# Row loads that wait for products alone, stores one unit later, biases spread; four output buffers for the gated products

## The chip, the cores and the metric

The kernel runs on one NeuronCore of a Trainium2 chip. The metric is the device time of one execution in microseconds, the median of several runs. The core has five engines that matter here: TensorE (PE) multiplies, VectorE (DVE), ScalarE (ACT) and GpSimd (POOL) do elementwise work, and SyncE (SP) issues all the DMAs of this kernel on one queue. Each engine executes its own instructions in order, and engines wait for each other through semaphores.

## The reference, cut to what matters

The program is one transformer-like layer on 2 x 1024 tokens of width 2048: attention, a gated product with a context, and a large dense product. Two parts of it matter here.

```python
# gated products (the "mlp" stage): g_in, u_in are [tokens, 512], mlp_in_w is [2, 2048, 512]
gate = jnp.einsum('bli,oi->blo', g_in, mlp_in_w[0])
up = jnp.einsum('bli,oi->blo', u_in, mlp_in_w[1])
mlp_out = jax.nn.silu(gate) * up
...
# dense product (the "ffn" stage): x is [2, 1024, 2048], w is [2048, 2048]
w = _dequant(weight_q, scale, zp)          # (q - zp) * scale by groups of 64
x = x + jnp.einsum('bsk,nk->bsn', _layernorm(x), w) + bias
```

All of it is float32. The kernel splits each operand into a rounded high half and the remainder as low half, and forms three products (high by high, high by low, low by high) instead of one.

## The kernel before, in words

The stages follow each other in one program: qkv, attention, write1, the gated products (`build_mlp`, line 2186), write2 (`build_write2`, line 1714) and the dense product (`build_ffn`, line 2473). `build_plane` (line 2407) has no time of its own: it dequantises the weights of the dense product on DVE during the gated products. Each stage gives functions for each engine, and `build_rest` writes them out in order, so that the order on every engine is fixed by hand. Tail and head of two stages overlap through functions with `ahead` in their names.

**Gated products.** There are 64 units. A unit takes 512 tokens (a chunk of four tiles) and 128 output columns, and does 24 matmuls of 128x512: 12 into `psG` (gate) and 12 into `psU` (up), line 2325. Eight units (KS) make a chunk; four chunks are done with the first eight column blocks, then the same four with the other eight. So "chunk 3" below is units 24 to 31. In unit u:

- ACT makes `sil` from `psG` (L2284), then the high halves of rows (`hi_x`, L2258) and weights (`hi_w`, L2247).
- DVE multiplies `psU` by `sil` into `mo` (L2385). This instruction waits until the buffer `mo[u % 2]` is stored, which is the store of unit u-2. Behind it in DVE's queue stand the low halves (`lo_x` L2263, `lo_w` L2251) and the dequantisation of `build_plane` (L2442, L2447, L2455).
- SP's loop (line 2334) goes once per unit: it issues the loads of weights and of rows (`raw`, four tiles for the next chunk, asked for in units 1 to 4 of a chunk, and split by ACT and DVE in the same units 1 to 4), the loads and stores of `build_plane` every third unit, and at the end waits for `mo` of this unit and stores it (L2352).

**Dense product.** A Strassen-like scheme: seven products (steps) of half-size blocks for each of two groups of columns, 14 steps of eight units (`PAIRS`), 112 units in all. Units 0 to 7 are mixed into the tail of write2, units 8 to 111 follow (`SEAM` = 8). One unit is 24 matmuls of 128x512 into `psF[u % 2]` (L2904 to L2906). The rows of a unit are one block or the sum or difference of two blocks of the normalised input; five of the seven steps (1, 2, 4, 5, 6) have two blocks. For such a unit:

- SP loads the first block into `xl[u % 4]` (L2598) and the second into `xs[i % 3]` (L2605), and pieces of the next step's weights (L2615, and L2620 where two are added);
- POOL adds the two blocks (L2859), and two pieces of weights (L2868);
- ACT makes the high half into `xh[u % 3]` (L2738), DVE the low half (`lo_x`, L2787), and the same for pieces (L2748, L2792);
- PE multiplies; DVE adds the product to one or two accumulators (`finish`, L2802, one add for each output cell of the unit).

The order on DVE in iteration u is `finish(u-1)`, `lo_x(u+2)`, pieces. PE starts unit u after `lo_x(u)` and `finish(u-2)`. An accumulator (cell) starts from the residual `x` plus bias: SP loads the residual (`load_base`, L2632), POOL adds the bias (`with_bias`, L2852) three iterations later. After its last unit the cell is stored to `y` (L2639). `base_at` says in which iteration each cell's residual is loaded. SP's loop in this stage (line 2706) sets the order of everything:

```python
for u in range(SEAM, UNITS):
    sp.wait_ge(y_ok, adds[u + 1])      # finish(u) on DVE is done
    ...                                # stores of cells whose last unit is u
    if u + 4 < UNITS:
        load_x(sp, u + 4)              # itself waits for mm_ok, unit u's product
        load_second(sp, u + 4)         # waits for the low half of three sums before
    ...                                # pieces of weights, then residuals
```

Of the kernel before, what the change touches and what calls it, by code (L numbers as in the profile page):

```python
# [19 lines left out]
ALU = mybir.AluOpType  # L20
# [1705 lines left out]
def build_write2(nc, io, k, zone, mlp, stored, cleared):  # L1726
# [8 lines left out]
    with ExitStack() as ctx:  # L1735
# [87 lines left out]
        def scalar_ahead(act, i):  # L1823

            if i == 0:
                act.wait_ge(mlp["mm_u"], 7 * KS)
                act.wait_ge(stored["w_out"], 16 * stored["groups"])
                act.wait_ge(stored["d_out"], 16 * stored["groups"] // 2)
            act.wait_ge(w_in[i % RW], 16 * (i // RW + 1))
            act.activation(wh[:, i * PT:(i + 1) * PT], wraw[:, i % RW], ACT.Copy).then_inc(w_hi, 1)  # L1830

        def vector_ahead(dve, i):

            if i == 0:
                dve.wait_ge(mlp["mm_u"], 7 * KS)
                dve.wait_ge(stored["w_out"], 16 * stored["groups"])
                dve.wait_ge(stored["d_out"], 16 * stored["groups"] // 2)
            if i == RW:
# [346 lines left out]
def build_mlp(nc, io, k, zone, w1, plane):  # L2185


    UNITS = CHUNKS * KM
    with ExitStack() as ctx:
# [5 lines left out]
        mo = sb("m_mo", [P, 2, CH * P])  # L2195
# [16 lines left out]
        mo_out = [sem(f"mo_out{p}") for p in range(2)]  # L2212
# [3 lines left out]
        made = tuple(range(4, 4 + 3 * C * KH, 3))  # L2216

# [115 lines left out]
        def sync(sp, load_w2, load_y):  # L2333
            for u in range(UNITS):
                if u + 4 < KS:
                    load_weights(sp, u + 4)
                if u < UNITS - KS and 1 <= u % KS <= CH:
                    load_reads(sp, CH * (u // KS + 1) + u % KS - 1)
# [13 lines left out]
                sp.dma_start(dst, mo[:, u % 2].rearrange("p (t j) -> p t j", j=P)).then_inc(mo_out[u % 2], 16)  # L2352
            for p in range(2):
                sp.wait_ge(mo_out[p], 16 * UNITS // 2)

# [4 lines left out]
        def scalar(act, hi_w2, hi_y):  # L2360
            for u in range(UNITS):
# [4 lines left out]
                if u < UNITS - KS and 1 <= u % KS <= CH:  # L2366
                    hi_x(act, CH * (u // KS + 1) + u % KS - 1)
# [10 lines left out]
        def vector(dve, lo_w2):  # L2378
            lo_w(dve, 2)
            for u in range(UNITS):  # L2380
                dve.wait_ge(sil_ok, u + 1)
                dve.wait_ge(mm_u, u + 1)
                if u >= 2:
                    dve.wait_ge(mo_out[u % 2], 16 * (u // 2))
                dve.tensor_tensor(mo[:, u % 2], psU[u % 2][:], sil[:, u % 2], ALU.mult).then_inc(mo_ok, 1)  # L2385
                if u + 3 < KS:
                    lo_w(dve, u + 3)
                if u < UNITS - KS and 1 <= u % KS <= CH:
                    lo_x(dve, CH * (u // KS + 1) + u % KS - 1)
# [10 lines left out]
                for i in ahead.get(u, ()):  # L2400
# [3 lines left out]
                    scalar_ahead=scalar_ahead, gpsimd_ahead=gpsimd_ahead, mm_u=mm_u, mo_ok=mo_ok, x_lo=x_lo, w_lo=w_lo)  # L2404


def build_plane(nc, io, k, zone):
# [4 lines left out]
    with ExitStack() as ctx:  # L2412
# [4 lines left out]
        sz = sb("p_sz", [P, RING, 2, H])  # L2417
        diff = sb("p_diff", [P, KH // 2, H])
        q_in = [sem(f"q_in{p}") for p in range(RING)]
# [52 lines left out]
def build_ffn(nc, io, k, zone, w2):  # L2472
# [46 lines left out]
    for j in range(PAIRS):  # L2519
        base_at[0, 0, 1, j] = base_at[0, 1, 1, j] = j - 2 * PAIRS  # L2520
        base_at[0, 0, 0, j] = j + 4
        base_at[0, 1, 0, j] = j + 14
        for half, n in ((0, 1), (1, 0), (0, 0), (1, 1)):
            base_at[1, half, n, j] = last_unit[0, half, n, j] + (4 if (half, n) == (0, 1) else 2)
# [582 lines left out]
```

## Time and profile before

| | us |
|---|---|
| median of 3 runs | 2405.39 |
| lowest, highest | 2388.42, 2405.92 |
| the profiled execution | 2406.18 |
| its span in the trace | 2404.4 |

The profile is of one execution. Busy time is time in which an engine executes; the granted clock of TensorE (PEclk) is given as a share of 2.4 GHz. "Waits" are idle times before an instruction, put down to what ended them. In the chain of waits one walks back from the last instruction to whatever released it. The gated products last from 945.8 to 1349.8 us, units 8 to 111 of the dense product from 1696.2 (start of unit 8) to 2400.6 us (end of unit 111).

### The profile page before, as it was taken

The page shows a single profiled execution, that of the slowest core. Times are in us where ns is not written, and L with a number is a line of the kernel's source. Part 1 is how long each engine was busy: PE and PEld are TensorE (multiplying, and loading weights), DVE is VectorE, ACT ScalarE, POOL GpSimd, SP SyncE. Part 2 cuts the span into 40 slices and gives each one's busy share as a digit, 9 for nine tenths or more (in the row PEclk, how much of TensorE's full clock was granted, in tenths as well). Part 3 has the DMA queues.
Part 4 walks back from the last instruction along what each step waited for, and adds up shares of the span by engine and source line. Part 5 has one row for each costly group of instructions (what it writes and reads, how often), then busy time and mean ns, then how long its engine had stood idle before and what let it go on. Part 6 is the DMA issues. An engine that isn't in the chain of part 4 may idle for free.

```text
span 2404.4 us, 34634 instructions
## 1 busy us (share of the span) xinstructions
PE 2168.2 (90%) x11176; PEld 1745.4 (73%) x11176; DVE 1439.1 (60%) x1950; ACT 1087.3 (45%) x1700; POOL 1179.3 (49%) x717
## 2 busy tenths in 40 slices
PE   6899989999979998997899999998889888989887
PEld 5777756666668887875677889996667666768666
DVE  7778767777647885443544277678545544545443
ACT  3444458888856777221212356665222222222221
POOL 0111159999977775000000387866683675352552
PEclk9999979999988998998899999999999999999999
DMA  5778653333336654766777568789885887675784
GB/s 176 234 239 255 222 148 100 102 93 104 78 104 235 218 209 167 249 210 214 250 246 258 186 254 302 301 292 320 278 286 185 264 279 240 212 258 180 244 258 149
DMA packets 259628, 516.93 MB, mean 215 GB/s; under 512 B 20978, under 2 KB 136690, under 8 KB 240964
## 3 DMA queue, kind: packets, MB, share of 16 engines
q1 hardware_dynamic: 259524, 515.60, 65.3%
q8 instruction: 58, 0.95, 0.2%
q14 instruction: 46, 0.38, 0.0%
HBM read 359.81 MB, written 155.45 MB: 214 GB/s over the span
## 4 chain that ended last, share of the span: by engine, by line
PE 45%; DMA 20%; DVE 13%; issue 7%; ACT 6%; POOL 5%; SPq 4%; DVEq 0%; ACTq 0%; POOLq 0%
DMA s_f_xs<-xnT 9%; PE s_w_psA L1903 5%; PE s_w_psB L1903 5%; DMA s_m_raw<-giT 4%; PE s_psO L922 4%; DMA s_q_xc<-xP 4%; PE s_psS L868 4%; POOL s_f_xs L2859 3%; PE s_m_psG L2325 3%; PE s_m_psU L2325 3%; PE s_psF L2904 3%; PE s_psF L2906 3%; PE s_psF L2905 3%; PE s_psX L899 3%; DMA mlpT<-s_m_mo 2%
## 5 line engine op out<-in xcount | busy, mean ns | idle before, releaser
L2859 POOL TENSOR_TENSOR s_f_xs<-s_f_xl,s_f_xs 128x1024 f32<-128x1024 f32 x80 | 194.5, 2432 | 303.6 <-DMA s_f_xs<-xnT 303.6
L1053 POOL TENSOR_TENSOR s_a_pl<-s_a_pf,s_a_ph 128x1024 fp32r<-128x1024 f32 x128 | 301.9, 2393 | 21.8 <-ACT s_a_pf L1010 21.7
L2787 DVE TENSOR_TENSOR s_f_xl<-s_f_xs,s_f_xh 128x1024 fp32r<-128x1024 f32 x80 | 102.8, 1286 | 306.0 <-ACT s_f_xh L2738 306.0
L2073 POOL TENSOR_TENSOR s_w_yl<-s_w_y,s_w_yh 128x1024 fp32r<-128x1024 f32 x32 | 76.0, 2399 | 414.6 <-ACT s_w_yh L1983 414.6
L2738 ACT ACTIVATE s_f_xh<-s_f_xs 128x1024 fp32r<-128x1024 f32 x80 | 84.8, 1060 | 421.5 <-POOL s_f_xs L2859 421.5
L948 DVE TENSOR_REDUCE s_a_mx<-s_psS 128x1 f32<-128x512 f32 (+2 forms) x248 | 179.3, 754 | 97.2 <-PE s_psS L876 96.7
L2904 PE MATMUL s_psF<-s_f_wh,s_f_xh 128*128 128x512 f32 x448 | 184.1, 411 | 48.0 <-DVE s_f_acc L2802 40.3
L2905 PE MATMUL s_psF<-s_f_wl,s_f_xh 128*128 128x512 f32 x448 | 181.8, 406 | 0.0
L2906 PE MATMUL s_psF<-s_f_wh,s_f_xl 128*128 128x512 f32 x448 | 181.6, 405 | 0.0
L1007 ACT ACTIVATE s_a_ph<-s_psX 128x1024 fp32r<-128x1024 f32 (+1 forms) x160 | 150.6, 941 | 51.5 <-PE s_psX L904 47.8
L449 POOL TENSOR_TENSOR s_q_qk<-s_q_ra,s_q_rb 128x1024 f32<-128x1024 f32 x16 | 37.8, 2360 | 270.7 <-DVE s_q_rb L692 270.7
L2802 DVE TENSOR_TENSOR s_f_acc<-s_f_acc,s_psF 128x512 f32<-128x512 f32 x192 | 124.0, 680 | 45.1 <-PE s_psF L2906 44.9
L2904 PEld LDWEIGHTS s_psF<-s_f_wh,s_f_xh 128*128 128x128 f32 x448 | 87.1, 194 | 79.7 <-issue 45.6
L2904 PE MATMUL s_psF<-s_f_whB,s_f_xh 128*128 128x512 f32 x336 | 136.0, 405 | 3.6 <-DVE s_f_wlB L2792 3.6
L922 PE MATMUL s_psO<-s_a_ph,s_a_vs 128*65 128x512 f32 (+3 forms) x384 | 128.4, 350 | 7.4 <-POOL s_a_pl L1053 7.4
L2905 PE MATMUL s_psF<-s_f_wlB,s_f_xh 128*128 128x512 f32 x336 | 135.0, 402 | 0.0
L2906 PE MATMUL s_psF<-s_f_whB,s_f_xl 128*128 128x512 f32 x336 | 134.9, 401 | 0.0
L1010 ACT ACTIVATE s_a_pf<-s_psX 128x1024 f32<-128x1024 f32 x128 | 131.0, 1023 | 0.0
L2852 POOL TENSOR_TENSOR s_f_acc<-s_f_acc,s_f_fb 128x512 f32<-128x512 f32 x64 | 112.2, 1766 | 36.5 <-DMA s_f_acc<-x 24.8
L868 PE MATMUL s_psS<-s_a_k,s_a_q 96*128 96x512 f32 x372 | 116.4, 401 | 10.3 <-DVE s_a_mx L948 10.0
L922 PE MATMUL s_psO<-s_a_pl,s_a_vs 128*65 128x512 f32 (+3 forms) x384 | 125.3, 338 | 0.0
L2385 DVE TENSOR_TENSOR s_m_mo<-s_m_psU,s_m_sil 128x512 f32<-128x512 f32 x64 | 44.1, 689 | 99.9 <-DMA mlpT<-s_m_mo 42.7
(335 smaller groups left out, 6337.9 us busy)
## 6 DMA issues: line engine op xcount, KB each, us to landing
s_f_xl<-xnT SPq DMA_DIRECT2D x112, 512.0 KB, 5.2
s_f_xs<-xnT SPq DMA_DIRECT2D x80, 512.0 KB, 6.4
s_q_xt<-xT SPq DMA_DIRECT2D x16, 1024.0 KB, 7.7
s_q_xc<-xP SPq DMA_DIRECT2D x16, 1024.0 KB, 9.7
hsD<-s_q_hs SPq DMA_DIRECT2D x16, 1024.0 KB, 4.9
s_w_hin<-hsD SPq DMA_DIRECT2D x16, 1024.0 KB, 5.0
hs<-s_w_res SPq DMA_DIRECT2D x16, 1024.0 KB, 3.9
s_m_raw<-giT SPq DMA_DIRECT2D x32, 512.0 KB, 5.9
```

The costliest lines, as they stand in the source:

```text
L868: pe.matmul(psS[:, at:at + n], qa[0:K3, p, qi * P:(qi + 1) * P], ka[0:K3, p, kk:kk + n], start=True, stop=not last)
L922: mm = pe.matmul(psO[0:VW, half, 512 - n:512], vs[:, r, ki, :], part[:, r, at:at + n], start=(ki == 0 and part is ph), stop=(ki == (3, 7)[ ...
L948: dve.tensor_reduce(mx[:, slot % 2, qi:qi + 1], psS[:, off:off + (qi + 1) * P], AX, ALU.max).then_inc(mx_ok, 1)
L1007: act.activation(ph[:, r, at:at + wide[j]], src, ACT.Exp, scale=scale).then_inc(exp_ok, 1)
L1010: act.activation(full, src, ACT.Exp, scale=scale).then_inc(exp_ok, 1)
L1053: pool.tensor_tensor(pl[:, r, cols], pf[:, j - 1], ph[:, r, cols], ALU.subtract).then_inc(pl_ok, 1)
L1903: mm = pe.matmul(bank[:, 0:n], a[:, p, kt], b[:, kt, cols], start=False, stop=(kt == KM - 1 and a is yl))
L2325: mm = pe.matmul(bank[u % 2][:], a[:, kt], b[:, :, kt], start=(i == 0 and a is w[m][0] and b is xh), stop=(i == KH - 1 and a is w[m][1]))
L2859: pool.tensor_tensor(xs[i % 3][:], xl[u % 4][:].bitcast(F32), xs[i % 3][:], ALU.add if product(u)[1][1][2] > 0 else ALU.subtract).then_inc ...
L2904: pe.matmul(out[:], xh[u % 3][:, kt], high(q, kt), start=(kt == 0), stop=False)
L2905: pe.matmul(out[:], xh[u % 3][:, kt], low(q, kt), start=False, stop=False)
L2906: mm = pe.matmul(out[:], xl[u % 4][:, kt], high(q, kt), start=False, stop=(kt == HK - 1))
```

## The change

In the gated products `mo` becomes four buffers instead of two for units 0 to 51 (`WIDE`), of which two lie in the region of `build_plane`, whose small buffer `p_sz` moves; the last 12 units use two. ACT's and DVE's first use of that region in write2 waits for the stores from these two buffers. Rows for the next chunk are asked for in units 0, 1, 3, 4 of a chunk and split in units 2, 3, 5, 6.

In the dense product SP's iteration u first issues the rows of unit u+4 and the pieces, then waits for `finish(u-1)`, stores the cells whose last unit is u-1, and loads residuals. `base_at` is given anew: the residuals of cells (0,1,0,j) are asked for in iteration 21+j instead of 14+j, and those of group 1 in 45+j, 51+j, 54+j and 77+j instead of 12+j, 50+j, 42+j and 34+j. The ring of semaphores of residuals goes from 8 to 6 and that of stores from 4 to 3. The bias row is loaded ahead of the first two residuals.

```diff
@@ build_write2, scalar_ahead and vector_ahead (the same two lines in each)
                 act.wait_ge(stored["d_out"], 16 * stored["groups"] // 2)
+                for out in mlp["spare_out"]:
+                    act.wait_ge(out, 16 * mlp["spare"])
@@ build_mlp
     UNITS = CHUNKS * KM
+    WIDE = UNITS - 12
...
-        mo = sb("m_mo", [P, 2, CH * P])
+        mo = [sb(f"m_mo{n}", [P, CH * P]) for n in range(2)]
+        mo += [shelf(nc, "s4_", zone["E"] + (28 + 2 * n) * 1024, zone["end"])(f"m_mo{n + 2}", [P, CH * P]) for n in range(2)]
...
-        mo_out = [sem(f"mo_out{p}") for p in range(2)]
+        mo_out = [sem(f"mo_out{p}") for p in range(4)]
+
+        asked, split = (0, 1, 3, 4), (2, 3, 5, 6)
...
+        def place(u):
+
+            return u % 4 if u < WIDE else u % 2
+
+        sent = [0]
+        for u in range(UNITS):
+            sent.append(sum(place(v) == place(u + 1) for v in range(u + 1)))
@@ build_mlp, sync
-                if u < UNITS - KS and 1 <= u % KS <= CH:
-                    load_reads(sp, CH * (u // KS + 1) + u % KS - 1)
+                if u < UNITS - KS and u % KS in asked:
+                    load_reads(sp, CH * (u // KS + 1) + asked.index(u % KS))
...
-                sp.dma_start(dst, mo[:, u % 2].rearrange("p (t j) -> p t j", j=P)).then_inc(mo_out[u % 2], 16)
+                sp.dma_start(dst, mo[place(u)][:].rearrange("p (t j) -> p t j", j=P)).then_inc(mo_out[place(u)], 16)
@@ build_mlp, scalar (and vector alike, with lo_x)
-                if u < UNITS - KS and 1 <= u % KS <= CH:
-                    hi_x(act, CH * (u // KS + 1) + u % KS - 1)
+                if u < UNITS - KS and u % KS in split:
+                    hi_x(act, CH * (u // KS + 1) + split.index(u % KS))
@@ build_mlp, vector
-                if u >= 2:
-                    dve.wait_ge(mo_out[u % 2], 16 * (u // 2))
-                dve.tensor_tensor(mo[:, u % 2], psU[u % 2][:], sil[:, u % 2], ALU.mult).then_inc(mo_ok, 1)
+                if sent[u]:
+                    dve.wait_ge(mo_out[place(u)], 16 * sent[u])
+                dve.tensor_tensor(mo[place(u)][:], psU[u % 2][:], sil[:, u % 2], ALU.mult).then_inc(mo_ok, 1)
@@ build_plane
-        sz = sb("p_sz", [P, RING, 2, H])
         diff = sb("p_diff", [P, KH // 2, H])
+        sz = shelf(nc, "s7_", zone["E"] + 36 * 1024, zone["end"])("p_sz", [P, RING, 2, H])
@@ build_ffn
-        base_at[0, 1, 0, j] = j + 14
-        for half, n in ((0, 1), (1, 0), (0, 0), (1, 1)):
-            base_at[1, half, n, j] = last_unit[0, half, n, j] + (4 if (half, n) == (0, 1) else 2)
+        base_at[0, 1, 0, j] = 3 * PAIRS + j - 3
+        base_at[1, 0, 1, j] = STEPS * PAIRS + j - 11
+        base_at[1, 1, 1, j] = STEPS * PAIRS + j - 5
+        base_at[1, 0, 0, j] = STEPS * PAIRS + j - 2
+        base_at[1, 1, 0, j] = (STEPS + 3) * PAIRS + j - 3
...
-    RB, RY, RW = 8, 4, 5
+    RB, RY, RW = 6, 3, 5
@@ build_ffn, sync_ahead, i == 1
+                sp.dma_start(fb[0][:].rearrange("p c n -> p (c n)"), io["fbias"][:, 0:2 * H]).then_inc(fb_in, 16)
                 load_base(sp, bases[0])
                 load_base(sp, bases[1])
-                sp.dma_start(fb[0][:].rearrange("p c n -> p (c n)"), io["fbias"][:, 0:2 * H]).then_inc(fb_in, 16)
@@ build_ffn, sync
-            for u in range(SEAM, UNITS):
-                sp.wait_ge(y_ok, adds[u + 1])
-                for cell in touched(u):
-                    if last_unit[cell] == u:
-                        store(sp, cell)
+            for u in range(SEAM, UNITS + 1):
                 if u + 4 < UNITS:
                     load_x(sp, u + 4)
                     load_second(sp, u + 4)
-                for n in pieces(u):
-                    load_piece(sp, n)
+                if u < UNITS:
+                    for n in pieces(u):
+                        load_piece(sp, n)
+                if u > SEAM:
+                    sp.wait_ge(y_ok, adds[u])
+                    for cell in touched(u - 1):
+                        if last_unit[cell] == u - 1:
+                            store(sp, cell)
                 for cell in bases[24:]:
                     if base_at[cell] == u:
                         load_base(sp, cell)
             for r in range(RY):
-                sp.wait_ge(y_out[r], 16 * len(stores) // RY)
+                sp.wait_ge(y_out[r], 16 * len(range(r, len(stores), RY)))
```

## Rows read from the trace of the kernel before

**Rows 1.** The page, part 1: busy time, share of the span and instructions by engine

```profile
PE 2168.2 (90%) x11176; PEld 1745.4 (73%) x11176; DVE 1439.1 (60%) x1950; ACT 1087.3 (45%) x1700; POOL 1179.3 (49%) x717
```

**Rows 2.** Waits of PE and DVE, gated products (940 to 1355 us): total, times, longest

```profile
PE s_m_psG L2325 <- ACT s_m_sil L2284: 29.3, 7, 13.0
...
DVE s_m_mo L2385 <- DMA mlpT<-s_m_mo: 42.7, 7, 9.4
```

**Rows 3.** Chain of waits in the gated products: start, us, what

```profile
1110.34 12.00 DMA s_m_raw<-giT
...
1148.44 11.69 DMA mlpT<-s_m_mo
```

**Rows 4.** Windows, gated products: us, PE, PEld, DVE, ACT, POOL busy, PEclk, DMA share, GB/s

```profile
994.50:1038.00 43.50, 43.50 (x194) 36.02 (x193) 23.26 (x18) 8.81 (x12) 0.00 (x0) 1.00 0.69 228
1038.00:1084.50 46.50, 44.06 (x193) 35.87 (x192) 20.96 (x18) 8.46 (x12) 0.00 (x0) 1.00 0.67 212
1084.50:1208.70 124.20, 97.28 (x386) 77.87 (x386) 57.54 (x47) 24.71 (x32) 0.00 (x0) 0.88 0.73 239
1208.70:1306.30 97.60, 89.52 (x386) 72.97 (x385) 46.23 (x38) 17.04 (x24) 0.00 (x0) 0.98 0.69 229
```

**Rows 5.** Waits of PE in the dense product (1696 to 2404 us)

```profile
PE s_psF L2904 <- DVE s_f_acc L2802: 72.8, 40, 5.2
```

**Rows 6.** Chain of waits in the dense product, one turn of the loop

```profile
2112.55 0.34 SPq L2639
...
2112.93 0.43 SPq L2598
...
2113.40 6.07 DMA s_f_xs<-xnT
...
2119.60 2.40 POOL s_f_xs L2859
...
2122.02 1.07 ACT s_f_xh L2738
...
2123.11 0.86 DVE s_f_xl L2787
...
2124.26 0.68 DVE s_f_wl L2792
2124.94 1.21 DVE s_f_acc L2802 x2
```

**Rows 7.** Windows, dense product: the same columns as rows 4

```profile
1696.20:1817.40 121.20, 98.22 (x388) 75.25 (x386) 58.89 (x55) 28.14 (x34) 95.91 (x52) 0.94 0.82 273
1817.40:1862.20 44.80, 44.80 (x194) 35.90 (x193) 24.56 (x32) 13.27 (x17) 9.87 (x5) 1.00 0.53 175
1862.20:2036.30 174.10, 147.96 (x577) 114.66 (x576) 83.29 (x90) 39.62 (x48) 110.45 (x57) 0.93 0.81 262
2036.30:2081.10 44.80, 44.80 (x193) 36.10 (x193) 28.02 (x32) 12.66 (x16) 13.26 (x7) 1.00 0.63 204
2081.10:2187.60 106.50, 94.22 (x386) 73.31 (x386) 49.93 (x59) 27.10 (x32) 58.02 (x30) 0.97 0.74 247
2187.60:2232.80 45.20, 44.80 (x194) 35.78 (x192) 24.25 (x30) 12.65 (x16) 5.04 (x2) 1.00 0.45 151
2232.80:2400.60 167.80, 141.46 (x576) 108.94 (x576) 68.91 (x81) 33.46 (x38) 75.26 (x38) 0.98 0.74 224
```

**Rows 8.** The same view for units 8 to 11 alone

```profile
1696.20:1728.80 32.60, 26.03 (x100) 20.25 (x97) 13.41 (x13) 6.88 (x9) 18.65 (x11) 0.90 0.84 291
```

**Rows 9.** Tile xs in the dense product: issue to landing of its loads and others

```profile
DMA to landing us min/median/max: 4.5/6.4/9.1
```

**Rows 10.** POOL in one unit of step 2, in order of time

```profile
1791.84 1.28 POOL L2868 TENSOR_TENSOR s_f_ws<-s_f_wl,s_f_ws 128x512 f32<-128x512 f32 x1
1793.09 3.97 POOL L2852 TENSOR_TENSOR s_f_acc<-s_f_acc,s_f_fb 128x512 f32<-128x512 f32 x2
```

**Rows 11.** DMA issues: count, KB each, median us to landing

```profile
s_f_acc<-x SPq DMA_DIRECT2D x64, 256.0 KB, 6.9
```

More of the change, by code:

```diff
@@ L1837, in vector_ahead @@
                 dve.wait_ge(stored["d_out"], 16 * stored["groups"] // 2)
+                for out in mlp["spare_out"]:
+                    dve.wait_ge(out, 16 * mlp["spare"])
             if i == RW:
@@ L2351, in sync @@
                 dst = io["mlpT"].rearrange("t p f -> p t f")[:, CH * chunk:CH * (chunk + 1), ds((KS * half + m) * P, P)]
-                sp.dma_start(dst, mo[:, u % 2].rearrange("p (t j) -> p t j", j=P)).then_inc(mo_out[u % 2], 16)
+                sp.dma_start(dst, mo[place(u)][:].rearrange("p (t j) -> p t j", j=P)).then_inc(mo_out[place(u)], 16)
             for p in range(2):
-                sp.wait_ge(mo_out[p], 16 * UNITS // 2)
+                sp.wait_ge(mo_out[p], 16 * (WIDE // 4 + (UNITS - WIDE) // 2))
+                sp.wait_ge(mo_out[2 + p], 16 * WIDE // 4)
         def tensor(pe):
@@ L2382, in vector @@
                 dve.wait_ge(mm_u, u + 1)
-                if u >= 2:
-                    dve.wait_ge(mo_out[u % 2], 16 * (u // 2))
-                dve.tensor_tensor(mo[:, u % 2], psU[u % 2][:], sil[:, u % 2], ALU.mult).then_inc(mo_ok, 1)
+                if sent[u]:
+                    dve.wait_ge(mo_out[place(u)], 16 * sent[u])
+                dve.tensor_tensor(mo[place(u)][:], psU[u % 2][:], sil[:, u % 2], ALU.mult).then_inc(mo_ok, 1)
                 if u + 3 < KS:
                     lo_w(dve, u + 3)
-                if u < UNITS - KS and 1 <= u % KS <= CH:
-                    lo_x(dve, CH * (u // KS + 1) + u % KS - 1)
+                if u < UNITS - KS and u % KS in split:
+                    lo_x(dve, CH * (u // KS + 1) + split.index(u % KS))
                 if 1 <= u - (CHUNKS - 1) * KS < KS:
@@ L2403, in build_mlp @@
         return dict(sync=sync, tensor=tensor, scalar=scalar, vector=vector, sync_ahead=sync_ahead, tensor_ahead=tensor_ahead,
-                    scalar_ahead=scalar_ahead, gpsimd_ahead=gpsimd_ahead, mm_u=mm_u, mo_ok=mo_ok, x_lo=x_lo, w_lo=w_lo)
+                    scalar_ahead=scalar_ahead, gpsimd_ahead=gpsimd_ahead, mm_u=mm_u, mo_ok=mo_ok, x_lo=x_lo, w_lo=w_lo, spare_out=mo_out[2:], spare=WIDE // 4)
 def build_plane(nc, io, k, zone):
```

## The prediction

> **What bounds the kernel now.** I read the page first: TensorE is busy for 90% of the span and nothing else for over 73% [rows 1]. That points to PE, but PE busy is not PE at its rate, so the next view is the windows, cut at the units' own borders. In the dense product the steps whose units load a single block of rows take 44.8 us for eight units, with PE busy all the time at clock 1.00: 5.6 us a unit is PE's own rate there. The steps with two blocks take 121.2 us for two steps, 174.1 for three, 106.5 for two and 167.8 for three, 569.6 us for ten steps or 7.12 us a unit [rows 7]. So 569.6 - 10 x 44.8 = 121.6 us lie above PE's rate. In the gated products an undisturbed chunk takes 43.5 us, and units 8k to 8k+7 of chunks 3 and 4 together 124.2 instead of 87 [rows 4].
>
> The third view says who holds PE. In the dense product PE waits 72.8 us in 40 waits for `finish` on DVE [rows 5], but an add of 0.6 us is not slow: the chain of waits shows what it stands behind. One turn goes: store of `y` 0.34, load of rows 0.43, landing of the second block 6.07, sum on POOL 2.40, high half on ACT 1.07, low half on DVE 0.86, piece 0.68, `finish` 1.21, and then SP issues again, 13.6 us after the turn began [rows 6]. It serves two units: `finish(u)` stands on DVE behind `lo_x(u+2)`, SP asks for the rows of unit u+4 only after `finish(u)`, and these must be through `lo_x(u+4)` before `finish(u+2)`. A turn of 13.6 us for two units is 6.8 a unit, where PE needs 5.6. This latency loop, not the rate of any engine, bounds the two-block steps. The rest of the 121.6 us, beside the waits, is PE at the lower clock after stalls (0.93 to 0.98 in these windows, 1.00 in the others) [rows 7].
>
> In the gated products PE waits for `sil` 29.3 us, and DVE waits 42.7 us in seven waits for the store of `mo` two units before [rows 2]. The chain alternates between two transfers, loads of `raw` and stores of `mo`, which take up to 12.0 and 11.7 us to land [rows 3]; a unit is 5.44 us.
>
> **The change, part by part: gated products.** Four buffers: `mo(u)` waits for the store of u-4, issued three to four units (16 to 22 us) before, against a landing of up to 11.7 [rows 3]. The wait goes for units up to 51; from unit 52 it is back to two units (10.9 us), and a late store can still cost 1 to 2 us. Rows of the next chunk are split two units later than asked for: issue just after `mo(u-1)`, `hi_x` behind the gate of unit u+2, so 2.5 units or 13.6 us against 12.0. What was behind the stalled DVE instruction (SP's wait for `mo`, hence its next loads) comes free with it. What is late next: in chunk 3 SP's load of weights waits for `lo_w` of two before, and `hi_w` uses it one and a half units after. And the DMA engines: chunks 3 and 4 moved 239 GB/s x 124.2 us = 29.7 MB at a busy share of 0.73, so 327 GB/s at full share [rows 4]; the same bytes need 91 us, more than PE's 87. I take 97 for the two (bounds 91 and 124). The 46.5 us of chunk 2 become 44, the 97.6 us of chunks 5 and 6 become 89 [rows 4]. Gain 27.2 + 2.5 + 8.6 = 38 us; bounds 10 (only the stores' waits outside chunk 3 go) and 48. DVE and ACT do the same work. The moved buffer and the waits in write2 cost nothing: they are for stores landed four units before.
>
> **Dense product, the loads.** SP now asks for unit u+4 when product u ends. It needs 0.43 issue + 6.4 landing (the median, [rows 9]) + 2.40 + 1.07 + 0.86 [rows 6] and some 0.3 between, 11.5 us, and has three units, 16.8 us. The loop is cut, with 5.3 us to spare: landings up to 11.7 us are hidden, and the longest of before was 9.1 [rows 9]. SP's new wait, `finish(u-1)` at the end of iteration u, has queued behind it the stores of u-1, the residuals, and the loads of iteration u+1. These last need product u+1, later than `finish(u-1)` in any case, so it costs nothing while `lo_x(u+1)` is in time. A store one unit later costs nothing: the accumulator's next residual comes at least two iterations after it. The tail keeps its order (last product, `finish`, store): 0.
>
> **The residuals spread.** In step 2 two residuals came per unit, and POOL did 2.40 for the sum [rows 6], 1.28 for the piece and 3.97 for two biases [rows 10], 7.65 us per unit against PE's 5.6: there POOL itself was the bound. With none of them in step 2, POOL has 3.7. They now stand in steps with one block of rows, where POOL is idle most of the time (9.87 busy in 44.8, [rows 7]), and in steps 5 and 6, where sum, bias of 2.0 and at most one piece make 5.7. The first use of a cell is three to eleven units after its load; a landing of 6.9 [rows 11] is hidden. The ring of six: in write2's last tile the seventh residual waits for the first to land, which holds the four pieces and the rows behind it for 0 to 2 us; the queue drains meanwhile, and I take 0.5 against a bias row about 1 us earlier: 0 together.
>
> **What the bytes allow.** I counted the DMAs SP issues per step: of units loading two blocks, 2 x 0.52 MB of rows, up to two pieces of 0.26 and one store of 0.26, 1.84 MB a unit; residuals before made it 2.10. For steps 1 to 13 of the new order this is 14.4, 11.0, 10.2, 14.4, 14.9, 13.6, 11.5, 14.4, 11.0, 10.2, 14.4, 13.6, 6.3 MB. The windows give between 224/0.74 = 303 and 273/0.82 = 333 GB/s at full share [rows 7]. At 303 the heavy steps need 47.5 to 49.2 us, at 333 43 to 45. I take the low end, since they come near full share. Three light steps (2, 9, 13) at 46, three of 14.4 MB (4, 8, 11) at 48, step 5 at 50, two of 13.6 at 46.5: 138 + 144 + 50 + 93 = 425. Step 1 keeps its first four units, 32.6 us [rows 8]: their rows are asked for before this loop or fall in the crowd of the stage's end; the other four take 5.7 each: 55.4. Together 480.4 against 569.6, a gain of 89.2; bounds 70 (28 lost to the DMA engines and new stalls) and 112 (all at PE's rate but step 1's head).
>
> The Trainium skill would have it otherwise. By "HBM Reference", section "Specifications (TRN2)", a core has about 358 GB/s of HBM bandwidth; 1.84 MB in 5.6 us is 329 GB/s, so the DMA engines would bind in no step. The heavy steps would then be at 46 like the light ones, an estimate of 11 us less in all. The trace stands against it with 303 to 333 at full share [rows 7].
>
> **Sum.** 2406.2 (the profiled execution's own time) - 38 - 89.2 = 2279; it lies 0.8 above the median of the runs, so 2278 against 2405.4.
>
> **The rivals.**
> - A, the DMA engines cap it: no group of steps has held more than 273 GB/s [rows 7]. If 280 were all they can hold, 14.4 MB need 51.4, 14.9 MB 53.2, 13.6 MB 48.6: 18 us more, and chunks 3 and 4 need 106, 9 more: 2305. At 260 GB/s (held by the ten steps on the mean) nearly 2340. For it: landings grow with the crowd. Against: shares of 0.74 to 0.82, not 1.
> - B, in the gated products the loop through weights takes the place of the one removed: SP waits for `lo_w`, `hi_w` for the landing, and chunk 3 stays as it is. The gain there is 10: 2306. For it: 12.0 us landing [rows 3] against 8 us of lead. Against: behind a late `hi_w` PE still has over a unit in hand.
> - C, slower: with loads asked for up to three units ahead, more of them share the engines and each lands later. It is slower than before only when (landing + 5.1)/3 exceeds 7.12 us, a landing of 16.3 where the median was 6.4; at 18 a unit takes 7.7, 80 units 46 us more, and without the gated products' gain 2452. Against: the bytes are fewer in the crowded steps, and the same engines carried 1.84 MB per turn of 6.8 us.
> - D, the store wait still holds SP in some place I have not seen, and the change does nothing: 2405.
>
> **How the numbers follow.** Forecast (2255 to 2295) 0.60; A 0.22; B 0.10; C 0.03; D 0.05. A measurement of this kernel tells about 1% from no change, 24 us. Forecast, A and B are faster by more than 1%: 0.92; D within: 0.04 and a hundredth of it slower with C: 0.04. The range takes the best case (48 + 112 lies at 2246) nearly whole and A up to 2325: 2250 to 2325.
>
> **What would show it.** Right: windows of two-block steps of 46 to 50 us with clock 1.00; PE's waits for `finish` in the dense product under 20 us, from 72.8; SP's loads of rows within 1 us of a product's end; median landing of `xs` up from 6.4 to 7 to 9; no DVE wait for stores of `mo` before unit 52; chunks 3 and 4 in 97 us; DMA share 0.9 or more in heavy steps; the kernel outside both stages unchanged to 3 us. Wrong: landings over 12 us with PE still waiting 50 us (A); waits of ACT for `wraw` in chunk 3 (B); PE waiting at POOL's biases in steps 0 of the second group, where they now stand.

## The result and the profile after

| | before | after |
|---|---|---|
| median, us | 2405.65 | 2254.32 |
| lowest, highest | 2388.42, 2412.37 | 2246.93, 2257.58 |
| runs | 4 | 4 |
| the profiled execution | 2406.18 | 2254.39 |
| its span | 2404.4 | 2252.3 |

The ratio is 0.9377, with a 95% interval of 0.9323 to 0.9431: 151 us faster, where 127 had been forecast. The time lies inside the range and just below the forecast's own (2255 to 2295).

The page of the changed kernel, part 1 and the first line of part 4, answers [rows 1]:

```profile
PE 2123.3 (94%) x11176; PEld 1724.2 (77%) x11176; DVE 1452.6 (64%) x1950; ACT 1087.4 (48%) x1700; POOL 1180.6 (52%) x717
...
PE 69%; DVE 10%; DMA 8%; issue 5%; ACT 5%; POOL 2%; SPq 1%; DVEq 0%; ACTq 0%; POOLq 0%
```

The instruction counts are those of before; nothing was removed but waiting. The chain that ends last is now PE for 69% and DMA for 8%; on the page of before those two stood at 45% and 20%.

**Where the 152 us of span went.** The start of the gated products came 2.7 us earlier (945.8 to 943.1), they take 355.3 us instead of 404.0 (48.7 less), from their end to the first unit of the dense product it is 283.1 against 283.0, units 0 to 7 take 63.8 against 63.4, and units 8 to 111 take 603.4 instead of 704.4 (101.0 less). So the kernel outside the two stages is unchanged to 3 us, and the two stages gained more than forecast by 10.7 and 11.8 us.

**Gated products.** The windows of chunks 0, 1, 3, 4, 5, 6 and 7 in the changed kernel, with the columns of [rows 4]:

```profile
943.10:993.70 50.60, 48.40 (x200) 39.42 (x201) 17.89 (x19) 20.80 (x30) 0.00 (x0) 0.93 0.54 175
993.70:1037.30 43.60, 43.60 (x194) 36.09 (x194) 23.25 (x18) 8.58 (x12) 0.00 (x0) 1.00 0.73 237
1080.80:1124.30 43.50, 43.50 (x193) 36.03 (x192) 30.05 (x25) 14.49 (x18) 0.00 (x0) 1.00 0.91 306
1124.30:1167.80 43.50, 43.50 (x193) 36.05 (x192) 26.50 (x21) 10.79 (x14) 0.00 (x0) 1.00 0.98 341
1167.80:1211.30 43.50, 43.50 (x193) 36.04 (x192) 22.18 (x18) 8.58 (x12) 0.00 (x0) 1.00 0.85 271
```
```profile
1211.30:1254.80 43.50, 43.50 (x193) 36.03 (x193) 24.45 (x20) 8.58 (x12) 0.00 (x0) 1.00 0.74 248
1254.80:1298.30 43.50, 43.50 (x193) 36.03 (x193) 18.45 (x22) 17.27 (x19) 4.76 (x2) 1.00 0.65 214
```

Seven of the eight chunks are at 43.5 us with PE busy all the time and the clock at 1.00, including chunks 3 and 4, which stood at 124.2 us together with the clock at 0.88 [rows 4]. The row to remember is the fourth: 341 GB/s at a DMA share of 0.98, and PE without a stall.

The waits of PE and DVE in the gated products (940 to 1305 us) of the changed kernel answer [rows 2]; DVE has more rows, of these the first two and the store's:

```profile
PE s_m_psG L2341 <- issue: 4.5, 1, 4.5
PE s_w_psT L1389 <- DVE s_w_yn L1647: 2.1, 1, 2.1
```
```profile
DVE s_m_mo L2402 <- issue: 105.7, 44, 4.5
DVE s_m_mo L2402 <- PE s_m_psU L2341: 37.2, 10, 4.8
...
DVE s_p_diff L2472 <- DMA wD<-s_p_diff: 8.5, 2, 5.0
```

PE's wait for `sil` is gone, and so is DVE's wait for the store of `mo`. DVE still idles before `mo`: 37.2 us of it end with the product, which is PE's own pace, and to 105.7 us the profile puts no releaser ("issue"). Transfers did not get quicker. The tiles `raw` and then `mo`, issue to landing, same stretch, answer [rows 3]:

```profile
DMA to landing us min/median/max: 3.6/5.8/10.7
...
DMA to landing us min/median/max: 2.3/5.2/12.1
```

A store that takes 12.1 us still happens; with four buffers it no longer ends a wait.

**Dense product.** The windows of steps 1, 2, 4, 5, 6 and 12 in the changed kernel, then of all units 8 to 111; columns as before, they answer [rows 7]:

```profile
1645.30:1702.40 57.10, 48.97 (x194) 37.91 (x193) 29.89 (x29) 13.65 (x17) 44.48 (x22) 0.94 0.89 313
1702.40:1749.00 46.60, 45.23 (x192) 35.90 (x193) 28.47 (x27) 15.14 (x18) 33.41 (x18) 1.00 0.81 260
1793.80:1838.40 44.60, 44.60 (x193) 35.94 (x192) 23.96 (x31) 12.38 (x15) 29.63 (x16) 1.00 0.94 311
1838.40:1884.30 45.90, 45.04 (x193) 35.83 (x192) 27.34 (x32) 13.44 (x17) 31.99 (x17) 1.00 0.97 321
1884.30:1933.00 48.70, 46.52 (x194) 37.05 (x193) 33.13 (x27) 13.92 (x18) 34.84 (x18) 0.96 0.91 300
2158.20:2203.90 45.70, 44.87 (x193) 35.86 (x192) 29.47 (x32) 12.83 (x17) 31.36 (x17) 1.00 0.95 322
...
1645.30:2248.70 603.40, 588.95 (x2498) 469.61 (x2496) 348.69 (x374) 167.02 (x201) 367.75 (x189) 0.99 0.83 276
```

The heavy steps 4, 5 and 12 are within about 1 us of PE's 44.8 while the DMA engines are busy for 0.94 to 0.97. What is left above PE's rate stands in step 1 (12 us), step 2 (2) and step 6 (4).

The waits of PE (1645 to 2252 us) answer [rows 5], those of SP show who releases it, and the last line, tile `xs` from issue to landing, answers [rows 9]:

```profile
PE s_psF L2925 <- DVE s_f_acc L2823: 11.9, 8, 3.8
```
```profile
SPq L2617 <- PE s_psF L2927: 271.8, 79, 7.1
...
SPq L2658 <- DVE s_f_acc L2823: 28.6, 21, 5.2
```
```profile
DMA to landing us min/median/max: 4.5/6.8/11.1
```

SP's load of rows (L2617) now stands 79 times behind a product. The rows of a two-block unit u+4 are asked for 0.03 to 0.08 us after the end of product u, but for units 12 and 13 (4.6 and 0.9 us); before it was 7.9 us at the median and 14.2 at most. The landing's median rose only from 6.4 to 6.8, its longest from 9.1 to 11.1, which the prediction's 11.7 still covers.

### The profile page after: what moved, and what is told of

The parts are those of the page before. It is cut to its first block, busy times and chain, and to the rows that moved or that the text cites. A ratio compares the mean times of both kernels' runs of the same rounds, so it can differ in the third digit from the quotient of the medians.

```text
span 2252.3 us, 34615 instructions
## 1 busy us (share of the span) xinstructions
PE 2123.3 (94%) x11176; PEld 1724.2 (77%) x11176; DVE 1452.6 (64%) x1950; ACT 1087.4 (48%) x1700; POOL 1180.6 (52%) x717
## 4 chain that ended last, share of the span: by engine, by line
PE 69%; DVE 10%; DMA 8%; issue 5%; ACT 5%; POOL 2%; SPq 1%; DVEq 0%; ACTq 0%; POOLq 0%
PE s_m_psG L2341 8%; PE s_m_psU L2341 8%; PE s_psF L2925 7%; PE s_psF L2926 7%; PE s_psF L2927 7%; PE s_w_psA L1907 5%; PE s_w_psB L1907 5%; PE s_psO L922 4%; DMA s_q_xc<-xP 4%; PE s_psS L868 4%; PE s_psX L899 3%; DVE s_a_mx L948 1%; DMA s_f_xs<-xnT 1%; PE s_w_psT L1939 1%; PE s_w_psR L1406 1%
## 5 line engine op out<-in xcount | busy, mean ns | idle before, releaser
L2880 POOL TENSOR_TENSOR s_f_xs<-s_f_xl,s_f_xs 128x1024 f32<-128x1024 f32 x80 | 203.7, 2546 | 165.4 <-DMA s_f_xs<-xnT 165.4
L2077 POOL TENSOR_TENSOR s_w_yl<-s_w_y,s_w_yh 128x1024 fp32r<-128x1024 f32 x32 | 76.1, 2404 | 365.9 <-ACT s_w_yh L1987 365.9
L2925 PE MATMUL s_psF<-s_f_wh,s_f_xh 128*128 128x512 f32 x448 | 178.7, 399 | 9.7 <-DVE s_f_acc L2823 8.6
L2300 ACT ACTIVATE s_m_sil<-s_m_psG 128x512 f32<-128x512 f32 x64 | 38.2, 597 | 228.8 <-PE s_m_psG L2341 228.7
L2873 POOL TENSOR_TENSOR s_f_acc<-s_f_acc,s_f_fb 128x512 f32<-128x512 f32 x64 | 102.4, 1612 | 69.5 <-DMA s_f_acc<-x 69.4
L2402 DVE TENSOR_TENSOR s_m_mo<-s_m_psU,s_m_sil 128x512 f32<-128x512 f32 x64 | 44.1, 690 | 143.0 <-issue 105.7
```

Source lines behind the costliest of these rows:

```text
L2880: pool.tensor_tensor(xs[i % 3][:], xl[u % 4][:].bitcast(F32), xs[i % 3][:], ALU.add if product(u)[1][1][2] > 0 else ALU.subtract).then_inc ...
L2925: pe.matmul(out[:], xh[u % 3][:, kt], high(q, kt), start=(kt == 0), stop=False)
```

## The experiments

Two theories on why the time fell further than forecast. **Latency**: both stages were bound only by how early a transfer was asked for; the DMA engines have no limit near these loads, so that once nothing waits, everything goes at PE's rate. **Rate** (the prediction's term, and rival A): the engines give out at 303 to 333 GB/s, and the heavy steps stay above PE's rate for it. The runs also ask which part of the change brought what. Stage times are read from the windows of each run: the stages ahead, which no experiment touches, scatter (the gated products start between 943 and 954 us), so a window is sharper than a whole time. A window scatters too: the changed loop of the dense product took 598.1 to 603.4 us for units 8 to 111 in the five traces that have it (the change and runs 2, 5, 6 and, but for the place of the store, 7). So a difference under some 5 us in that stage tells nothing, unless it stands in one step that is alike in the others.

**1. The gated products alone.** The changed kernel with the dense product of before.

```diff
-            for u in range(SEAM, UNITS + 1):
+            for u in range(SEAM, UNITS):
+                sp.wait_ge(y_ok, adds[u + 1])
...                                 # and base_at, fb[0], stores as before; rings at 6 and 3
```

> The change in the gated products alone (the dense product as before, but with the two semaphore rings at 6 and 3). Theory: the two parts are independent; this keeps the gated products' 355 us and gives back the dense product's 100.8 us: 2254 + 101 = 2355. Rival (a faster stage before pushes the dense product into another crowd of transfers): outside 2345 to 2365. The smaller rings alone cost under 2 us.

2364.48 us (ratio 0.9827, 0.977 to 0.9884). The whole time is at the upper end of what was expected. The gated products take 353.0 us, units 8 to 111 706.0, with the smaller rings in them against 704.4 without. One stretch as long as a chunk (its end of chunk 3 and most of chunk 4) carried more than any in the changed kernel:

```profile
1124.00:1167.50 43.50, 43.50 (x193) 36.02 (x193) 26.38 (x24) 10.74 (x14) 0.00 (x0) 1.00 1.03 351
```

So the gated products' gain is this part's alone, and 351 GB/s, with the DMA engines busy without a gap (their share can read a little over 1), still does not slow PE.

**2. The dense product alone.** The kernel before with `build_ffn` of the changed one.

```diff
-        base_at[0, 1, 0, j] = j + 14
+        base_at[0, 1, 0, j] = 3 * PAIRS + j - 3
...                                 # all of build_ffn; build_mlp, build_plane as before
```

> The change in the dense product alone, gated products as before. Theory: 2254 + 48.7 = 2303, gated products 404 us, dense product from unit 8 about 604 us. Rival (the parts help each other): the two gains, this one's and that of the gated products alone, sum to less than 140 us instead of 151.

2300.76 us (0.9569, 0.9525 to 0.9613); units 8 to 111 take 599.0, the gated products 401.0, with chunks 3 and 4 at 122.0. By windows the parts alone gain 51.0 and 105.4 us in their own stages, the whole change 48.7 and 101.0: by these the two parts add, and neither needs the other. The expectation asked for whole times (under 140 us together would mean that they help each other), and these do not settle it: the two ratios give 145 us together where the whole change gave 150, the medians of that session (2399.03 for the kernel before) give 133, and the intervals of the two ratios are 14 and 11 us to each side.

**3. The loads wait for `finish` again.** Only SP's order is undone; residuals stay spread.

```diff
-            for u in range(SEAM, UNITS + 1):
+            for u in range(SEAM, UNITS):
+                sp.wait_ge(y_ok, adds[u + 1])
+                for cell in touched(u):
+                    if last_unit[cell] == u:
+                        store(sp, cell)
...                                 # and no wait for finish(u-1), no store behind the loads
```

> The changed kernel, but SP's loads of rows wait for finish(u) again, with the store ahead of them as before; residuals stay spread. Theory (the latency loop of 13.6 us per two units is the bound): nine two-block steps go back to 6.8 us a unit, 54 us a step instead of 45.6 on the mean, so 75 to 85 us slower than the changed kernel: 2329 to 2339, PE's waits for finish at 50 us or more. Rival (the spread residuals and their bytes did most of it): under 2290.

2336.71 us (0.9713, 0.9669 to 0.9756). Waits of PE from 1654 us on, the landings of `xs`, and the windows of steps 4 and 5:

```profile
PE s_psF L2923 <- DVE s_f_acc L2821: 65.5, 41, 5.3
```
```profile
DMA to landing us min/median/max: 4.5/6.3/8.4
```
```profile
1813.80:1864.20 50.40, 45.78 (x193) 35.42 (x192) 24.96 (x32) 11.90 (x15) 26.54 (x14) 1.00 0.83 271
1864.20:1920.80 56.60, 48.27 (x193) 36.59 (x193) 25.34 (x32) 13.55 (x16) 30.63 (x16) 0.97 0.83 262
```

With this one wait in SP's loop PE's waits are back (40 before, 41 here), though each transfer lands sooner than in the changed kernel (6.3 against 6.8) and the engines are busy for only 0.83. That is latency, not rate. Units 8 to 111 take 685.4: the order of the loads alone is worth 82.0 us of the stage.

**4. The residuals as before.** Only `base_at` is undone.

```diff
-        base_at[0, 1, 0, j] = 3 * PAIRS + j - 3
+        base_at[0, 1, 0, j] = j + 14
...                                 # and the four of group 1
```

> The changed kernel with the residuals asked for where they were before (14+j, 12+j, 50+j, 42+j, 34+j); loads wait for products alone. Theory: step 2 is bound by POOL at 7.65 us a unit, 61 us instead of 46.6; steps 4 and 5 carry 16.3 MB, at 333 GB/s 49 us instead of 44.6 and 45.9; step 6 2 us less: together 20 us slower, 2274. Rival (transfers capped at 303 GB/s, as the prediction took it): steps 4 and 5 at 54 us, 2283 or more. Rival (POOL's turns are hidden by the longer lead): under 2262.

2266.26 us (0.9425, 0.9387 to 0.9464); units 8 to 111 take 613.7, 10.3 more, of which 7.5 in step 2 and 4.5 in step 5. Windows of steps 2, 4 and 5, and the landings of `xs` in step 5:

```profile
1708.80:1762.90 54.10, 46.35 (x192) 35.52 (x193) 29.00 (x26) 14.39 (x17) 54.10 (x30) 1.00 0.78 278
1807.70:1852.30 44.60, 44.60 (x193) 35.78 (x192) 25.91 (x30) 11.85 (x14) 33.64 (x17) 1.00 0.96 331
1852.30:1902.70 50.40, 46.66 (x193) 35.45 (x192) 32.83 (x32) 13.56 (x16) 50.40 (x25) 1.00 1.01 345
```
```profile
DMA to landing us min/median/max: 5.9/6.7/7.4
```

In steps 2 and 5 POOL is busy for the whole window: 54.10 of 54.10 and 50.40 of 50.40. That is the bound that the prediction had worked out for step 2 (7.65 us a unit with two biases), though only part of the step has two: the four units 19 to 22 take 7.52 to 7.54 us each. In step 5 the DMA engines are full as well, at 345 GB/s; but the landings there are no longer than elsewhere (6.7), so it is POOL that holds this step. The expectation was too high by 8 us: it had step 2 at 61 us, as if all eight units had two biases, and it had put a price on the bytes of step 4 (49 us), which is at PE's rate at 331 GB/s.

**5. Two output buffers, rows as in the change.**

```diff
-            return u % 4 if u < WIDE else u % 2
+            return u % 2
...                                 # and the last waits for the stores, to match
```

> The changed kernel with mo in two buffers again, rows still asked for and split at the new places. Theory: the stores of mo were late because they stood among the loads in a crowd, and up to 12.1 us against 10.9 us of room; with rows early, DVE waits for a few stores, each stall partly taken up by the unit that PE has in hand: 3 to 12 us slower, 2257 to 2266. Rival (the two buffers were the main wait of that stage): 25 us or more slower.

2262.13 us (0.9394, 0.9339 to 0.9449). The gated products take 364.3 us, 9.0 more. The stall of 8.5 us at unit 32 and 2.5 us after it cost 11.0; against that chunk 0 took 48.6 us here and 50.6 in the profile of the change. Chunk 0 does so with the same code too: 48.3 to 48.6 us in four traces, 50.3 to 50.6 in five. So the two buffers are worth 11.0. DVE's row of waits for the store (948 to 1313 us):

```profile
DVE s_m_mo L2401 <- DMA mlpT<-s_m_mo: 24.6, 5, 8.4
```

DVE waits 24.6 us in five waits and PE loses 11.0: the total of such a row is no price, since DVE has cover of its own. That holds for the 42.7 us in [rows 2] as well.

**6. Rows asked for and split as before, four buffers kept.**

```diff
-        asked, split = (0, 1, 3, 4), (2, 3, 5, 6)
+        asked, split = (1, 2, 3, 4), (1, 2, 3, 4)
```

> The changed kernel with four buffers, rows of the next chunk asked for and split in units 1 to 4 as before. Theory: raw rows land up to 12 us after issue and are wanted within half a unit, DVE and ACT stand on them, chunk 3 worst: 20 to 35 us slower, 2274 to 2289. Rival (the stores' wait was the main one): under 2262.

2292.16 us (0.9512, 0.9462 to 0.9562), 3 us beyond what was expected. The gated products take 390.2, 34.9 more, chunk 3 alone 65.5. PE's wait and two of ACT's (954 to 1345 us):

```profile
PE s_m_psG L2341 <- ACT s_m_sil L2300: 20.4, 7, 12.1
```
```profile
ACT s_m_xhXA L2274 <- DMA s_m_raw<-giT: 76.8, 12, 17.6
ACT s_m_xhXB L2274 <- DMA s_m_raw<-giT: 74.1, 16, 11.0
```

ACT waits for rows that have not landed, 17.6 us at the longest (7.0 and 0.4 in all in the changed kernel), and the next `sil` stands behind that `hi_x`. So of the change's two edits in this stage, the room between load and split did most (34.9), the buffers the smaller part (11.0).

The trace of before had the same waits of ACT (940 to 1355 us), about as long:

```profile
ACT s_m_xhXB L2258 <- DMA s_m_raw<-giT: 81.5, 16, 11.7
ACT s_m_xhXA L2258 <- DMA s_m_raw<-giT: 78.7, 12, 17.6
```

DVE stood behind these high halves for 54.0 and 51.4 us there, 14.9 at the longest, against the 42.7 us (9.4 at the longest) for stores that [rows 2] shows.

**7. Stores ahead of the loads.** SP waits for `finish(u-1)` and stores first, then asks for rows.

```diff
+                if u > SEAM:
+                    sp.wait_ge(y_ok, adds[u])
+                    ...                    # stores
                 if u + 4 < UNITS:
                     load_x(sp, u + 4)
...                                 # the same wait and stores are gone behind the pieces
```

> The changed kernel, but in each iteration SP first waits for finish(u-1) and stores the cells of u-1, then loads the rows of u+4 and pieces; residuals last as now. Theory: finish(u-1) is nearly always over when product u ends, so only the place in the queue changes: 0 to 4 us slower, 2254 to 2258. Rival (what matters is that 0.26 MB of store no longer stand ahead of the rows): 10 us or more slower.

2257.15 us (0.9363, 0.9308 to 0.9418), units 8 to 111 600.7: no difference. What mattered is which `finish` SP waits for, u-1 instead of u, not whether it stands before or after the loads.

**8. One unit less of lead.** When product u ends, SP asks for the rows of u+3 instead of u+4.

```diff
-                if u + 4 < UNITS:
-                    load_x(sp, u + 4)
-                    load_second(sp, u + 4)
+                if SEAM < u < UNITS - 3:
+                    sp.wait_ge(mm_ok, u + 1)
+                    load_x(sp, u + 3)
+                    load_second(sp, u + 3)
```

> The changed kernel, but iteration u issues the rows of unit u+3 instead of u+4, after product u. Theory: the way from issue to low half is 11.5 to 12.5 us at the median landing of 6.8 us, and the room is now two units, 11.2 us; so two-block units take on the mean 0.5 to 1.5 us more: 35 to 100 us slower, 2290 to 2355. Rival (the DMA engines' rate, not the lead, sets the remaining distance to PE's rate): under 2275.

2347.81 us (0.9741, 0.9683 to 0.9798). Waits of PE, the landings, and units 8 to 111:

```profile
PE s_psF L2926 <- DVE s_f_acc L2824: 70.5, 35, 5.1
```
```profile
DMA to landing us min/median/max: 4.4/6.3/11.2
```
```profile
1649.20:2345.50 696.30, 619.02 (x2499) 483.85 (x2497) 332.05 (x374) 166.73 (x201) 362.67 (x189) 0.95 0.74 239
```

92.9 us of the stage's 101 are gone with one unit of lead. The way of a pair of blocks took 11.5 us in the prediction's sum, and two units are 11.2: at two there is nothing to spare, at three 5.3 us. Between those two lies nearly the whole gain. This is the plainest evidence for latency: same bytes, same instructions, and a DMA share of 0.74.

**9 to 11. What is left, at the seam.** In step 1 of the changed kernel PE stalls 3.95 and 3.25 us at units 10 and 11 for rows asked for late, and units 13 to 15 take 6.15 to 6.29 us each. The timeline of POOL there, and of DVE beside it (start, us, instruction):

```profile
1681.63 2.86 POOL L2880 TENSOR_TENSOR s_f_xs<-s_f_xl,s_f_xs 128x1024 f32<-128x1024 f32 x1
1684.44 1.29 POOL L2889 TENSOR_TENSOR s_f_ws<-s_f_wlB,s_f_ws 128x512 f32<-128x512 f32 x1
1685.69 2.29 POOL L2873 TENSOR_TENSOR s_f_acc<-s_f_acc,s_f_fb 128x512 f32<-128x512 f32 x1
```
```profile
1685.61 1.23 DVE L2808 TENSOR_TENSOR s_f_xl<-s_f_xs,s_f_xh 128x1024 fp32r<-128x1024 f32 x1 [2.20 <-ACT s_f_xh L2759]
1686.75 1.77 DVE L2813 TENSOR_TENSOR s_f_wlB<-s_f_ws,s_f_whB 128x512 fp32r<-128x512 f32 x1
1688.45 1.27 DVE L2823 TENSOR_TENSOR s_f_acc<-s_f_acc,s_psF 128x512 f32<-128x512 f32 x2
```

POOL goes without a gap from 1681.63 to 1687.98, one sum, one piece, one bias: POOL bounds these units. Three kernels try both ends. The first adds the biases of group 0 earlier, out of these units, and loads the second bias row in iteration 28; the second asks for the rows of units 10 and 11 ahead of SP's wait for the last tile of write2; the third does both.

```diff
-            with_bias(pool, bases[16])
+            for b in range(16, 20):
+                with_bias(pool, bases[b])
...                                 # 20 to 23 in units 8 to 10
@@ sync_ahead, i == 3, out of i == 4 and sync
+                load_x(sp, 10)
+                load_second(sp, 10)
...
+                load_x(sp, 11)
+                load_second(sp, 11)
```

> The changed kernel; POOL adds the biases of the cells (0,0,0,j) earlier (four before unit 8's sums instead of one, two in iteration 8, one each in 9 and 10), and the second bias row is loaded in iteration 28 instead of ahead of unit 11's rows. Theory (POOL at 6.3 us a unit binds units 12 to 16): step 1 falls from 57.1 to 52 to 54, step 2 by about 1: 4 to 6 us faster, about 2249. Rival (DVE or the landings of 9 to 16 us in those units bind anyway): within 2 us of the changed kernel.

> The changed kernel, but the rows of units 10 and 11 are issued ahead of SP's wait for the last tile of write2 (about 9 us earlier). Theory: the stalls of 3.95 and 3.25 us before units 10 and 11 and the lower clock after them go: 7 to 11 us faster, 2244 to 2247, unless POOL at 6.3 us a unit takes part of it back: then 4 to 7. Rival (POOL binds from unit 10 on): under 3 us.

> Both of these edits together. Theory: they remove one bound after the other, so their gains add: 11 to 16 us faster than the changed kernel, 2238 to 2243, step 1 at 46 to 48 us. Rival (one of the two hides the other): no more than the better of the two alone.

| | median, us | ratio, 95% | units 8 to 111 | step 1 | step 2 |
|---|---|---|---|---|---|
| the change | 2254.32 | 0.9377, 0.9323 to 0.9431 | 603.4 | 57.1 | 46.6 |
| biases earlier | 2252.85 | 0.9382, 0.9341 to 0.9423 | 595.6 | 55.2 | 45.1 |
| rows earlier | 2245.28 | 0.9341, 0.9285 to 0.9398 | 594.6 | 51.4 | 46.6 |
| both | 2250.19 | 0.9368, 0.933 to 0.9405 | 592.0 | 51.1 | 44.6 |

Step 1, which takes 57.0 to 57.4 us in the five traces named above, is shorter by 1.9, 5.7 and 6.0 us, and step 2 by 1.5 us in the first and 2.0 in the third. Both bounds were where they were looked for: with the biases earlier units 13 to 15 take 5.60 to 5.67 us each (first and third kernel), with the rows earlier the stall at unit 10 is gone (second and third). The rest of the difference in units 8 to 111 can't be told from scatter: 592.0 to 595.6 against 598.1 to 603.4. The first and the third missed what was expected of step 1 (52 to 54 and 46 to 48), the third because unit 11 still stalls, 3.46 us. POOL in that kernel, in order of time:

```profile
1659.12 3.55 POOL L2874 TENSOR_TENSOR s_f_acc<-s_f_acc,s_f_fb 128x512 f32<-128x512 f32 x2
1662.63 2.39 POOL L2881 TENSOR_TENSOR s_f_xs<-s_f_xl,s_f_xs 128x1024 f32<-128x1024 f32 x1
1664.98 3.54 POOL L2890 TENSOR_TENSOR s_f_ws<-s_f_wlA,s_f_ws 128x512 f32<-128x512 f32 x2
```

The biases brought forward now stand ahead of the sum and the two pieces that unit 11 needs: the same work in another order on an engine without slack. They are not the whole cause. In the second kernel, which leaves the biases where they were, unit 11 stalls 3.10 us, and there POOL waits for the pieces to land:

```profile
1664.63 1.29 POOL L2889 TENSOR_TENSOR s_f_ws<-s_f_wlA,s_f_ws 128x512 f32<-128x512 f32 x1 [2.85 <-DMA s_f_ws<-wF]
1666.84 1.62 POOL L2889 TENSOR_TENSOR s_f_ws<-s_f_wlA,s_f_ws 128x512 f32<-128x512 f32 x1 [0.92 <-DMA s_f_ws<-wF]
```

No run moved the pieces, so how the stall at unit 11 divides between the two is open. Whether any of the three beats the change as a whole is not settled either: the medians of whole executions differ by 1.5 to 9 us, and the intervals overlap.

## Why the prediction was right, and where its size was off

**The reading of the bound held.** The dense product was bound by the latency loop through `finish`, not by an engine: putting the one wait back brings 82.0 of the stage's 101 us back (run 3). The forecast of its remedy held too, three units of lead against 11.5 us of way; run 8 shows that two are not enough. PE's waits for `finish` fell to 11.9 us (under 20 was predicted), the landings' median is 6.8 (7 to 9), the clock is 1.00 in steps 2, 4, 5 and 12 (0.94 in step 1 and 0.96 in step 6, behind their stalls), SP issues within 0.1 us of a product's end but for units 12 and 13, and there is no wait of `mo` for a store.

**The term that was mis-sized: the DMA rate, "I take the low end, since they come near full share".** The prediction read 303 to 333 GB/s out of [rows 7] and took 303. That was the quotient of one window, the last. The other six of [rows 7] give 323 to 336, and the busiest stretch, [rows 8], 291/0.84 = 346, so the range read was too narrow at the top and its low end was the exception. Near full share the runs measured 321 GB/s at 0.97, 322 at 0.95, 341 at 0.98, and 351 at 1.03 and 345 at 1.01 in runs 1 and 4: quotients of 331 to 348. At 330 the steps of 14.4 MB need 43.6 us and the one of 14.9 MB 45.2, so the other windows of before would have put them at PE's rate or within half a microsecond of it. By terms: steps 4, 8 and 11 took 44.6, 45.8 and 44.8, so 135.2 us instead of 144; step 5 took 45.9 instead of 50. These are 12.9 us under the forecast. The light steps 2, 9 and 13, which the rate did not price, took 136.6 instead of 138, so 14.3 in all.

The Trainium skill stated as much: by "HBM Reference", section "Specifications (TRN2)", a core has about 358 GB/s, and the heavy steps were to lie at 46 like the light ones. The measured 44.6 to 45.9 and the 351 GB/s are in line with it, though no run shows where the ceiling lies; the 303 that was preferred to it is not.

**Two terms were too good.** Step 1 took 57.1 instead of 55.4: its last three units go at POOL's 6.15 to 6.29 us, not at 5.7, because sum, piece and bias take 2.86, 1.29 and 2.29 there and not the 2.40, 1.28 and 2.0 of before. Steps 6 and 12 took 94.3 instead of 93. In step 6 that is one stall of 2.35 us at unit 52 and the lower clock behind it; ahead of it stand a landing of 10.1 us and a low half of a piece that took 2.86 us on DVE. It is no price of the residuals: with the same residuals runs 5, 6 and 7 have no stall there and step 6 at 44.7 to 44.9 us (run 2 has it at 46.6). With them the ten steps come to 469.1 against 480.4; the other 0.5 us of the 11.8 are in the single steps.

**Gated products: bytes and margin, not the rate.** Chunks 3 and 4 took 87.0, not 97. The 97 was a value between 91 (29.7 MB at 327 GB/s) and 124.2. Their windows now hold 306 and 341 GB/s for 43.5 us each, so 28.1 MB at 324 GB/s: the rate of 327 was right in size. Too high were the bytes, since these windows carry 1.6 MB less than the same chunks did (which transfers left them was not traced), and the 6 us added to the 91. Chunk 2 is at 43.5 (44 taken) and chunks 5 and 6 at 87.0 (89). Against that chunk 0 is 1.9 us longer, 50.6 against 48.7, which no step of the prediction had; it takes either time with the same code (run 5), so it is scatter, and chunks 1 to 7 alone gained 50.6. 10 + 0.5 + 2 - 1.9 = 10.6 us, the difference to 38 but for 0.1. The prediction priced the stage's two edits together, and of DVE's waits it named only the one for stores. Undone alone, the room between load and split was worth 34.9 and the buffers 11.0; both together are worth 50.6, so the two act on each other a little.

**Slips that moved nothing.** Rival A's aside that the ten steps held 260 GB/s on the mean should be 250, by the windows of [rows 7].

**The rivals.** A fell: where the engines are busiest, PE runs without a stall; its test, landings over 12 us with PE waiting 50, did not come. B fell: ACT does wait 18.6 us for `wraw`, 7.3 at most, but chunk 3 is at 43.5, so the unit in hand covered it. C needed landings of 16.3; the longest was 11.1. D fell with the 79 releases of SP by products.

**Residuals.** Spreading them is worth 10.3 us with the loads early (run 4). With the loads late it is worth about 19 (704.4 of before against 685.4 in run 3): the two parts hide a part of each other. The prediction priced neither alone.

## What to carry to other kernels

Count the way of a transfer (issue, landing, each conversion behind it) against the units between its issue and its use, and find which wait decides when it is asked for. When the way is just over a whole number of units, one more unit of lead can be worth nearly all of the loss, and a wait of the issuing engine for the youngest result costs that unit. A rate divided by the busy share of the DMA engines differs from window to window (303 to 346 GB/s here), and one low window is no ceiling: lay all of them side by side, with the busiest first, before a limit is put into the sum.

## What the runs showed of the hardware

- **The DMA engines hold 341 to 351 GB/s for 43.5 us** at shares of 0.98 and 1.03, and single transfers land later in it. Over the gated products of the changed kernel `raw` lands after 5.8 us at the median, in their crowded stretch (1080 to 1170 us) after 9.1, and PE does not stall there, because the rows are asked for early enough. In the dense product the median landing of `xs` goes from 6.3 us at a mean share of 0.76 (run 3, units 8 to 111) to 6.8 at 0.83, the longest from 8.4 to 11.1.
- **POOL and DVE stretch each other.** The bias add takes 1.26 us at its shortest and 2.29 beside DVE's `lo_x` and piece; the piece's low half on DVE 0.68 and 1.77; POOL's sum 2.40 and 2.86. By the Trainium skill, "SBUF — State Buffer", section "🔬 SBUF: two separate sides", a DVE instruction with two SBUF inputs and a GpSimd instruction that reads SBUF take turns at a shared port pair, one fully blocked while the other has it. The traces agree. In the dense product of the changed kernel 39 sums on POOL beside which DVE runs no instruction with two SBUF inputs take 2.37 to 2.41 us, 26 of them beside DVE's add that reads `psF`; the 40 beside one with two take up to 3.39. On DVE 43 low halves of pieces with POOL idle take 0.68 to 0.69, the 53 beside a POOL instruction up to 2.89, 1.78 at the median. It matters once stalls are gone: POOL went from cover to bound in the second half of step 1.
- **The clock followed the stalls.** It stood at 0.88 of 2.4 GHz on the mean in chunks 3 and 4 with stalls up to 13 us [rows 2, 4] (0.50, so 1.2 GHz, from 1123 to 1128 us, around the end of the longest) and is at 1.00 without them; over units 8 to 111 it is 0.99, against 0.98 in run 3 and 0.95 in run 8 with their stalls. So part of what a stall costs does not stand in the waits: of the 92.9 us that run 8 lost in the stage, 30.1 are in PE's busy time, which rose from 588.95 to 619.02 with the same matmuls.
